# The order of matmul pieces beside a selective scan: a third table of steps

## The reference, cut to what matters

```
h0 = per-sequence linear map of x (a 64x64 matrix chosen by an index) + bias
x, z = split(in_proj(h0));  xc = silu(causal conv of 4 taps (x))
dt_r, B, C = split(x_proj(xc));  delta = softplus(dt_proj(dt_r) + bias)
for every token t:   h = h * exp(delta_t * A) + (delta_t * xc_t) * B_t      # 1024 channels x 16 states
                     y_t = sum over the states of h * C_t
x1 = x + out_proj((y + xc * D) * silu(z))
x2 = x1 @ W.T + low-rank adapter(x1)
out = x1 + experts(x2), 4 of 16 experts per token, + one shared expert
```

## Time and profile before

| | us |
|---|---|
| median of 3 runs | 1859.88 (1859.28 to 1862.43) |
| the profiled execution | 1859.53 |
| its span | 1857.7 |
| DVE busy | 1453.7 (78%) |
| PE busy | 1641.9 (88%) |
| POOL busy | 1062.5 (57%) |
| ACT busy | 819.4 (44%) |

### The profile page before, as it was taken

How to read it: one execution, slowest core, us unless ns; L and a number is a source line. 1 busy time by engine, 2 the same in 40 slices (tenths; PEclk the granted TensorE clock), 3 DMA queues, 4 the chain that set the end, 5 groups by cost and what they waited for, 6 DMA issues and landing times. The chain is left out here.

```text
span 1857.7 us, 28398 instructions
## 1 busy us (share of the span) xinstructions
PE 1641.9 (88%) x7884; PEld 1200.2 (65%) x7884; DVE 1453.7 (78%) x1945; ACT 819.4 (44%) x1220; POOL 1062.5 (57%) x832
## 2 busy tenths in 40 slices
PE   8667867898997988887778999999989999999998
PEld 5255434555455655455454647778889999999997
DVE  3599999999999999999999933877455566565654
ACT  2656666566766567665655411000022233232322
POOL 0289579887599795797987671000044444344443
PEclk9868879999998999999978999999989999999999
DMA  5112212223323222331223243111156665666664
GB/s 129 36 59 69 59 40 72 66 80 97 68 86 108 80 80 80 91 98 57 74 65 119 84 153 124 68 69 52 54 141 151 161 164 135 169 137 146 151 176 70
DMA packets 130022, 181.92 MB, mean 98 GB/s; under 512 B 21443, under 2 KB 79555, under 8 KB 126788
## 3 DMA queue, kind: packets, MB, share of 16 engines
q1 hardware_dynamic: 109540, 131.85, 22.2%
q0 software_dynamic: 17888, 43.79, 12.1%
q10 hardware_dynamic: 2432, 4.33, 0.9%
HBM read 276.18 MB, written 37.36 MB: 169 GB/s over the span
## 5 line engine op out<-in xcount | busy, mean ns | idle before, releaser
L1194 POOL TENSOR_TENSOR arena_kept<-arena_kept,b_all 128x512 f32<-128x512 f32 x512 | 637.4, 1275 | 250.6 <-DVE arena_kept L1078 124.2
L1078 DVE TENSOR_TENSOR_SCAN arena_kept<-da,arena_kept 128x512 f32<-128x512 f32 x512 | 598.0, 1205 | 12.9 <-ACT da L927 9.4
L927 ACT ACTIVATE da<-arena_kept,a_neg 128x504 f32<-128x504 f32 x512 | 347.5, 684 | 245.6 <-DVE arena_kept L1078 239.4
L716 PE MATMUL hT<-ident_kept,arena_kept 128*128 128x128 f32 x2048 | 314.7, 301 | 143.8 <-DVE yacc L1090 89.3
L716 PEld LDWEIGHTS hT<-ident_kept,arena_kept 128*128 128x128 f32 x2048 | 257.4, 155 | 247.1 <-DVE arena_kept L1078 171.4
L1090 DVE SCALAR_TENSOR_TENSOR yacc<-hT,c_now,yacc 128x512 f32<-128x512 f32 x480 | 331.6, 733 | 4.6 <-PE hT L716 4.3
L2107 POOL DMA_INDIRECT out<-y,slots_kept x76 | 134.8, 1773 | 233.1 <-issue 174.4
L516 PE MATMUL bank<-hid,wt 128*128 128x512 f32 x512 | 239.1, 615 | 0.9 <-ACT hid L752 0.7
L516 PEld LDWEIGHTS bank<-hid,wt 128*128 128x128 f32 x512 | 98.6, 201 | 107.2 <-issue 105.1
L1977 ACT ACTIVATE gs<-egp 128x352 f32<-128x352 f32 x73 | 33.9, 464 | 238.3 <-PE eup L1287 237.7
L1739 POOL DMA_DIRECT2D slots_kept<-lists_kept x1 | 0.6, 567 | 212.3 <-DVE lists_kept L1691 212.3
(11 more groups left out here) (235 smaller groups left out, 3160.6 us busy)
## 6 DMA issues: line engine op xcount, KB each, us to landing
w_up_kept<-in_up_T SPq DMA_DIRECT2D x76, 1408.0 KB, 5.9
w_dn_kept<-in_dn_T SPq DMA_DIRECT2D x76, 768.0 KB, 7.2
b_all<-bt_scratch SPq DMA_DIRECT2D x128, 256.0 KB, 3.5
wt<-in_in_T SPq DMA_DIRECT2D x64, 256.0 KB, 3.0
wt<-in_out_T SPq DMA_DIRECT2D x32, 256.0 KB, 2.9
res<-in_x_pad SPq DMA_DIRECT2D x16, 256.0 KB, 3.7
x_scratch<-res SPq DMA_DIRECT2D x16, 256.0 KB, 2.2
wt<-in_w_T SPq DMA_DIRECT2D x16, 256.0 KB, 3.1
```

Source lines behind the costliest of these rows:

```text
L716: mm = nc.tensor.transpose(turned_in(j, m, t)[:, d * P:(d + 1) * P], h[:, m % RING, d, t * P:(t + 1) * P], ident[:])
L927: nc.scalar.activation(out[:, :, 1:], rows[:, :, 1:], ACT.Exp, scale=a_neg[:, d, n:n + 1]) \
L1078: nc.vector.tensor_tensor_scan(h[:, n % RING, i, :], da[i % RING][:], dbx[:, i, :], 0.0, ALU.mult, ALU.add).then_inc(scan_done, 1)
L1194: nc.gpsimd.tensor_tensor(dbx[:, i, :], u[:, d, :], b_all[:, m % RING, :], ALU.mult) \
```

## The change

Only the table changes. No instruction is added, removed or altered; the order of the pieces within the 32 steps of each block is another one.

```diff
 LINE = [
-    (["turn1", "gate4", "gate5"], []),
-    (["gate6", "z0"], ["cond0", "gate7"]),
-    (["out0"], []),
-    (["out1"], ["dt4"]),
-    (["out2"], []),
-    (["out3"], ["ln4", "cond1"]),
-    (["out4"], []),
-    (["out5"], ["dt5"]),
-    (["cond2"], ["ln5", "z1"]),
-    (["dt6"], ["dt7", "cond3"]),
-    (["ln6", "out6"], []),
-    (["out7"], []),
-    (["xr0", "x0"], ["skip0", "ln7"]),
-    (["x1", "z2"], []),
-    (["skip1", "xa", "x2"], ["xr1", "xr2"]),
-    (["x3"], ["skip2", "skip3"]),
+    (["turn1"], ["gate4", "gate5"]),
+    (["dt4", "gate6"], ["gate7", "z0"]),
+    (["dt5"], ["out0"]),
+    (["out1"], ["ln4"]),
+    (["out2"], ["cond0"]),
+    (["out3"], ["cond1"]),
+    (["out4"], ["ln5"]),
+    (["out5"], ["cond2"]),
+    ([], ["dt6", "cond3"]),
+    (["out6", "ln6"], []),
+    (["out7", "skip0"], []),
+    (["z1", "xr0"], ["dt7", "skip1"]),
+    (["xa", "ln7"], ["x0"]),
+    (["z2"], ["x1", "skip2"]),
+    (["x2", "skip3"], ["z3", "zsilu0"]),
+    (["x3"], []),
     (["turn0"], ["x4"]),
-    (["silu0"], ["x5", "z3"]),
-    (["x6"], ["zsilu0", "x7"]),
-    (["w0", "silu1", "rank0"], []),
-    (["rank1", "xr3"], ["dt0", "gate0"]),
-    (["w1"], ["gate1"]),
-    (["gate2", "w2"], ["ln0"]),
-    (["w3", "gate3"], ["row0", "dt1"]),
-    (["pre0", "bc0"], ["ln1"]),
-    (["z4"], ["bc1", "pre1"]),
-    ([], ["lg"]),
-    (["dt2"], ["ln2", "pre2", "row1"]),
-    (["z5"], ["dt3"]),
-    (["z6", "row2"], ["row3"]),
-    (["ln3", "pre3", "ct"], ["z7", "zsilu1"]),
+    (["x5"], ["silu0", "w0"]),
+    (["x6"], ["z4"]),
+    ([], ["x7", "gate0", "xr1"]),
+    (["w1", "gate1"], ["silu1", "rank0", "gate2"]),
+    (["xr2", "rank1"], ["dt0"]),
+    (["ln0", "w2"], ["gate3"]),
+    (["z5"], ["dt1"]),
+    (["ln1", "w3"], ["xr3"]),
+    (["z6"], ["dt2"]),
+    (["ln2", "lg"], ["row0"]),
+    (["row1", "row2"], ["z7"]),
+    (["row3", "pre0"], ["bc0", "pre1"]),
+    (["dt3"], ["pre2", "ln3", "bc1"]),
+    (["ct"], ["zsilu1", "pre3"]),
     ([], []),
 ]
```

## The result

The changed kernel is slower: 1865.85 us, the median of six runs (1862.46 to 1870.25), against 1859.07 (1855.45 to 1862.43) for six of the kernel before in the same session. The ratio is 1.0036, with a 95% interval of 1.0019 to 1.0052. I had forecast 1858.5, so this is the other side of "no change", at the time of rival 2 (1865). The profiled execution took 1864.6 us, 5.1 more than the one before, so 1.7 us of the 6.8 between the medians do not show in these traces.

The account below looks back on a forecast made before the run. DVE was taken to bound the scan, its 20.2 us of waits the whole stake for gain; -3.9 - 3.0 - 1.2 + 3.3 + 0.6 + 3.0 = -1.2 gave 1858.5 us, 8-in-10 range 1852 to 1865.5.

Parts of the forecast that it names:

- rival 2: PE becomes the bound in thin places, long second-list pieces at half clock costing up to 1.7 each: 1865 us, chance 0.20.
- Steps 17 to 20: Blocks 0 to 2: 2.6 us of excess goes, a new 1.3 wait for ACT comes in step 21; -3.9 in all.
- The block's end: End of step 31, blocks 0 to 2: DVE's waits for ACT's first decay all go, z7 being earlier; -3.0 us.
- zsilu0 in block 3: Block 3: the 1.18 us wait before step 20 goes, as the Silu moves to step 14's second list; -1.2 us.
- The row of B: Steps 3 to 5, blocks 1 to 3: out1 1.05 later behind out0, step 5 1.0 later; 1.1 a block, +3.3 us.
- xa: Step 12, three blocks: xa ends 7.2 into the step where DVE wants it at 7.1; +0.6 us.
- Late transposes: Long second-list pieces at half clock delay tile 3, mainly block 3: waits 7.3 us instead of 4.3, +3.0.
- signs of being wrong: Step 5 on time; L1090's PE waits under 3 or above 12 us; POOL wait at block head; difference outside scan.

Follow-up runs that it names:

- the repeat: The changed kernel once more with no edit, timed against the kernel before and traced a second time: 1867.39 us, ratio 1.0037.
- e1_out0: Changed kernel with out0 moved from the second list of step 2 back to its first, behind dt5: 1864.75 us, ratio 1.0021 to the kernel before.
- e10_out0: Kernel before with out0 moved from the first list of step 2 to its second: 1870.99 us, ratio 1.0061.

## Why the prediction was wrong

Its mechanisms were there; one term was put at a third of what the first trace has. The sum of the working, against that trace:

- **Steps 17 to 20, -3.9:** -0.7, -1.6 and -1.6 for blocks 0 to 2, -3.9. The sum is right; block 0 gave half, as its old wait in step 20 was 0.54 and not block 1's 1.07. It isn't safe, though: in the seven other traces that have this second half without repeats it is -0.6 to -4.2. In the repeat x4 stands behind the turn of step 16 and runs largely at the half clock (4.68 us), and the convolution of step 17 waits 1.7 for it.
- **The block's end, -3.0:** -2.8, and -2.4 to -3.2 in those seven. Partly for a reason I hadn't seen: the wait of 0.8 went, the copy of C fell by 0.6, and the six sums before it took 0.6 more (4.59 against 4.01).
- **zsilu0 in block 3, -1.2:** step 19 gave 1.26, step 15 took 0.85 back. -0.4.
- **The row of B, +3.3:** steps 4 to 8 cost 4.9, of which three late transposes in step 6 are 1.4; 3.5 is left (0.1, 1.6, 0.4 and 1.4 in blocks 0 to 3, where I had 0, 1.1, 1.1 and 1.1). Out1 started within 0.15 of the predicted time; the row of B was issued 0.76 later in its step than before, where I had 1.05. `e1_out0` takes the lateness of steps 4 to 8 away and `e10_out0` brings it into the old table, so the chain is shown. In the repeat this term is 5.2.
- **xa, +0.6:** step 12 is 0.8 longer in blocks 1 to 3, but step 14, 10.17 before, became a clean 9.33 in blocks 1 and 2. About 0, and for another reason than PE's end of `xa`: DVE has an instruction of that piece (L1033, 0.69 us, at 440.72 in step 14 before and at 429.61 in step 12 now), which moved along with it. So "in place of nothing" was wrong.
- **Late transposes, +3.0.** This is the step that failed: "My count is 2.2 + 1.3 (w0) + 1.2 (w2) + 0.3 for block 3's others, 1.3 for block 0, 1.0 for blocks 1 and 2 together: 7.3 instead of 4.3". Measured 13.5, +9.2, and 0.9 more that the trace books as waits of a scan for PE. By place: block 3 was about right in sum (6.3 against 5.0; w0 2.8 instead of 1.3). Blocks 1 and 2 have 5.7 where I put 1.0. I had looked for long pieces of the second list behind thin steps and let step 8 pass, whose second list holds only short ones: dt6 and cond3 are 2.9 us together at the full clock and 5.6 at the half, and out6, a first-list piece, then ran at the half clock too. In the repeat blocks 1 and 2 have 0.3, and the whole is 8.7, +4.4: there the term is off by 1.4 us, and the row of B by 1.9. My argument against rival 2, "blocks 0 to 2 have low stretches now and no such wait", told of the old order only. Rival 2 named this kind of wait rightly, but that its 13.6 and its 1865 were met is luck in part: it counted eight long second-list pieces at 1.7, while z0, which it named, cost nothing, and steps 9 and 10 paid for short pieces and for out6.

Two of the signs of being wrong came: L1090's waits for PE over 12 us (in the first trace, not in the repeat), and a difference outside the scan. The list that I started from left out the wait of the earlier trace rows: DVE's waits were 21.4 us in all and not 20.2.

The rule that I had weighed, from the Trainium skill's "TensorE: Matmul & The Clock Gate", section "What's actually happening", that activity lifts a default of low clock, stands; what I drew from it, fewer low stretches with pieces spread evenly, does not. The granted clock over the scan fell from 0.91 to 0.89 (0.90 in the repeat). Beside step 31 the new order has two empty first lists, steps 8 and 19, where the old had one, step 26; over the one of step 8 of block 1 the clock fell in both traces.

What the runs show of the whole: the loss lies in steps 0 to 16, 10.6 us by the ratio of two kernels, and steps 17 to 31 give back 4. That the half clock makes the waits of steps 9 to 11 is shown by the two traces of one kernel. How the median's 6.8 us divide between the clock and the row of B stays open: these two traces, with the same span, divide it as 7.0 and 4.9, and as 0.3 and 6.9. They also differ by 3 us outside the scan, for which I have no cause.

## What to carry to other kernels

When pieces are moved in an order that feeds a ring of engines, read for every gap on PE what comes behind it, the short pieces too, and price these at both clock levels: a place with a margin of 2 us at the full clock can have none at the half. Where a change has two halves in time, run each half with the other's old order; here that turned a loss of 0.36% into a gain of 0.21%, while mending the single places one by one gained nothing sure. And take a second trace of the same kernel before putting a gain of a few us at one place down to an edit: steps 9 to 11 of block 1 went from 25.2 to 21.6 us with z1 moved, and to 21.4 with nothing moved. And a queue that waits for one buffer holds back the urgent load behind it: a moved piece is also a moved wait there.

## What the hardware showed that I had not expected

- What stands ahead of a piece goes with its clock: out0 in the second list of step 2 takes 3.60 us behind z0 and dt5 in blocks 1 to 3 of five traces, and 4.85, 4.62 and 4.54 behind cond0 and transposes in the one trace of `e10_out0`.
- The same kernel's low stretches are not the same from run to run: dt6 at 397.93 took 1.92 us in one trace of the changed kernel and 1.43 in the other; single runs of it spread over 8 us, those of `e1_out0` over 15, the kernel before over 10 (1855.0 to 1865.12, 32 runs).
- The load of a row of B lands about 3.0 us after its issue at the least and 3.5 to 3.65 in the median of each of the 14 traces, but in each trace 5 to 10 of the 128 take more than 5, the longest 6.1 to 8.2.
- DVE's copy of C (128x64) takes 0.19 us with POOL idle. In the 24 copies, in ten traces, that began 0.27 us or more before the end of a POOL multiply it took 0.32 to 1.17 and ended 0.05 after that multiply. The Trainium skill, "SBUF — State Buffer", section "SBUF: two separate sides", has a port pair that DVE and GpSimd lock for a whole instruction, which agrees. DVE's scans ran beside POOL's multiplies at their usual 1.2 us: `da` lies in PSUM, so that a scan has one input in SBUF, and that section names a DVE instruction in a 2-port mode or with two SBUF inputs.
- Repeats that kept PE busy brought its clock in the scan to 0.96 and made the new table 24 us slower and the old one 39.
